# Queries of two pairs in one run, one E buffer of two tiles: a lambda convolution on Trainium2

## The reference

```python
softmax_keys = jax.nn.softmax(keys, axis=1)
values = _bn(xf @ Wv.T, gamma_v, beta_v, axes=(0, 2), ch_shape=(1, -1, 1))
queries = _bn(queries, gamma_q, beta_q, axes=(0, 2, 3), ch_shape=(1, -1, 1, 1))
content_lambda = jnp.einsum('bmk,bmv->bkv', softmax_keys, values)
position_lambdas = jnp.einsum('nmk,bmv->bnkv', E, values)
content_output = jnp.einsum('bknh,bkv->bhvn', queries, content_lambda)
position_output = jnp.einsum('bknh,bnkv->bhvn', queries, position_lambdas)
return (content_output + position_output).reshape(b, d, n1, n2)   # added to x
```

## Time and profile before

| | us |
|---|---|
| median of 3 runs | 1447.19 (1446.07 to 1447.33) |
| the profiled execution | 1447.59 |
| its span, first to last instruction | 1445.6 |
| TensorE busy | 1430.4 (99%) |
| VectorE busy | 852.0 (59%) |
| ScalarE busy | 757.0 (52%) |
| GpSimd busy | 424.6 (29%) |
| mean DMA rate | 93 GB/s |

### The profile page before, as it was taken

How to read it: one execution, slowest core, us unless ns; L and a number is a source line. 1 busy time by engine, 2 the same in 40 slices (tenths; PEclk the granted TensorE clock), 3 DMA queues, 4 the chain that set the end, 5 groups by cost and what they waited for, 6 DMA issues and landing times.

```text
span 1445.6 us, 36192 instructions
## 1 busy us (share of the span) xinstructions
PE 1430.4 (99%) x14608; PEld 1191.8 (82%) x14608; DVE 852.0 (59%) x1226; ACT 757.0 (52%) x1109; POOL 424.6 (29%) x366
## 2 busy tenths in 40 slices
PE   8999999999999999999999999999999999999998
PEld 7997888888888888888888888888888888888886
DVE  7989565555555555555555555555555555555553
ACT  6775555555455555554555455544555455545552
POOL 6683233223322332133212331233223322332130
PEclk9999999999999999999999999999999999999999
DMA  8845322434152422434152333424252333425221
GB/s 308 289 156 93 84 66 66 87 94 94 40 120 65 110 63 75 93 93 89 44 123 65 95 65 87 94 75 85 65 123 65 72 80 94 94 53 107 65 58 30
DMA packets 342684, 134.68 MB, mean 93 GB/s; under 512 B 206864, under 2 KB 338048, under 8 KB 342144
## 3 DMA queue, kind: packets, MB, share of 16 engines
q1 hardware_dynamic: 342656, 134.31, 38.6%
HBM read 109.12 MB, written 25.17 MB: 93 GB/s over the span
## 4 chain that ended last, share of the span: by engine, by line
PE 97%; DVE 1%; DMA 0%; issue 0%; ACT 0%; SPq 0%; POOL 0%; POOLq 0%; DVEq 0%
PE ps_a L1224 81%; PE ps_b L1241 5%; PE ps_a L1208 4%; PE ps_b L1104 3%; PE ps_a L1094 1%; PE ps_b L1163 1%; DMA x_main<-in_x 0%; DVE bn L719 0%; DVE q_stats L744 0%; DVE v_stats L738 0%; DVE key_diag L782 0%; POOL v_rstd L459 0%; PE ps_b L1179 0%; DVE top_level L774 0%; DVE top_level L773 0%
## 5 line engine op out<-in xcount | busy, mean ns | idle before, releaser
L1224 PE MATMUL ps_a<-v_hi,e_hi 128*128 128x512 f32 x1708 | 670.8, 393 | 0.0
L1224 PE MATMUL ps_a<-v_hi,e_lo 128*128 128x512 f32 x1708 | 664.7, 389 | 0.0
L657 ACT ACTIVATE q_diag<-q_blk,q_shift_n,q_scale_n 128x256 f32<-128x256 f32 x512 | 411.2, 868 | 42.9 <-PE ps_b L1241 42.9
L575 ACT ACTIVATE e_hi<-e_nat 128x512 fp32r<-128x512 f32 x305 | 192.8, 633 | 442.2 <-PE ps_a L1224 435.6
L1224 PE MATMUL ps_a<-b_lo,e_hi 128*128 128x512 f32 x976 | 379.6, 389 | 0.0
L1224 PEld LDWEIGHTS ps_a<-v_hi,e_hi 128*128 128x128 f32 x1708 | 320.5, 188 | 67.3
L1224 PEld LDWEIGHTS ps_a<-v_hi,e_lo 128*128 128x128 f32 x1708 | 320.7, 188 | 64.7
L486 POOL TENSOR_TENSOR e_nat<-e_nat,s_buf 128x512 f32<-128x512 f32 x61 | 79.7, 1306 | 920.2 <-DVE e_lo L749 920.2
L854 DVE TENSOR_TENSOR pos<-ps_a,content 128x512 f32<-128x512 f32 x183 | 126.6, 692 | 296.0 <-PE ps_a L1224 296.0
L749 DVE TENSOR_TENSOR e_lo<-e_nat,e_hi 128x512 fp32r<-128x512 f32 x305 | 290.7, 954 | 1.7 <-ACT e_hi L575 1.4
L1224 PE MATMUL ps_a<-t_lo,e_hi 128*128 128x512 f32 x732 | 285.4, 390 | 0.0
(11 more groups left out here) (133 smaller groups left out, 890.3 us busy)
## 6 DMA issues: line engine op xcount, KB each, us to landing
e_nat<-in_L_conv_E SPq DMA_DIRECT2D x128, 512.0 KB, 4.8
res<-in_x SPq DMA_DIRECT2D x64, 256.0 KB, 5.9
out_dram<-res SPq DMA_DIRECT2D x60, 256.0 KB, 4.7
x_main<-in_x SPq DMA_DIRECT2D x24, 512.0 KB, 6.0
q_dram<-q_nat SPq DMA_DIRECT2D x4, 2048.0 KB, 7.6
q_blk<-q_dram SPq DMA_DIRECT2D x32, 256.0 KB, 2.9
x_more<-in_x SPq DMA_DIRECT2D x8, 512.0 KB, 8.6
out_dram<-res SPq DMA_DIRECT2D x4, 192.0 KB, 3.7
```

Of the source, the lines that this page charges most:

```text
L575: nc.scalar.activation(e_hi[:, i], e_source(i, slot), ACT.Copy).then_inc(e_hi_ready, 1)
L657: ins = nc.scalar.activation(to[:, n], of, ACT.Identity, bias=q_shift_n[:, n:n + 1], scale=q_scale_n[:, n:n + 1])
L1224: ins = nc.tensor.matmul(BANK_OF[i], e[:, i, j].rearrange("p n k -> p (n k)"), v[:, j], start=(STARTS[i] and j == 0 and n == 0), stop=(STO ...
```

## The change

It runs the queries of pairs 2g and 2g+1 as one stretch of 128 matmuls (256 records), behind product 0 of pair 2g+2 (`query_group`), for g = 1 to 30. Queries 0, 1, 62 and the halves of 63 stay apart. For this `q_diag` and `pos` are held for two pairs, the sums are added with one instruction (`add_group`, from both banks of ps_b), and `res` is held for two groups of two pairs. To make room, `e_nat` shrinks from two slots to one: tile 1 of the next pair is loaded after split 5, tile 0 after split 6 (`next_e`), each with its own semaphore.

In odd pairs, where no query stands behind product 0, product 0 goes to bank_d and product 1 starts bank_a anew; VectorE adds product 0 into `head` and also, with content, into the two places of `pos` in which it is needed (two more additions). VectorE's and ScalarE's orders in a pair are changed: additions out of PSUM come ahead of splits, and a part of `norm_queries` ahead of each split. TensorE's loop now has two pairs in its body.

```diff
-        e_nat = sb("e_nat", [P, 2, 2 * TN, J * KD])
+        e_nat = sb("e_nat", [P, 2 * TN, J * KD])
-        res = sb("res", [P, G * NH, 2 * BN])
-        q_diag = sb("q_diag", [P, 2, B * NH * TN])
+        res = sb("res", [P, G * NH, 2, GN])
+        q_diag = sb("q_diag", [P, 2, 2, B * NH * TN])
-        pos = sb("pos", [P, 2, BV])
+        pos = sb("pos", [P, 2, 2, BV])
...
-        BANK_OF = (bank_a, bank_a, bank_b, bank_a, bank_c, bank_a, bank_b)
-        STARTS = (True, False, True, False, True, False, False)
+        BANK_OF = ((bank_a, bank_a, bank_b, bank_a, bank_c, bank_a, bank_b),
+                   (bank_d, bank_a, bank_b, bank_a, bank_c, bank_a, bank_b))
+        STARTS = ((True, False, True, False, True, False, False), (True, True, True, False, True, False, False))
...
+            def next_e(p):
+                sp.wait_ge(e_lo_ready, p * NP + NP - 1)
+                load_e(p + 1, 1)
+                sp.wait_ge(e_lo_ready, p * NP + NP)
+                load_e(p + 1, 0)
...
+            def even_loads(p, grp, half):
+                next_e(p)
+                sp.wait_ge(res_added, p)
+                store_res(grp - 1, 1 - half)
+
+            def odd_loads(p, grp, half, queries=True):
+                next_e(p)
+                sp.wait_ge(res_stored, grp * (16 * A))
+                load_res(grp + 1, 1 - half)
+                if queries:
                     sp.wait_ge(q_diag_ready, p + 1)
-                    load_q(blk * 2 + i // 2 + 2, i // 2)
+                    load_q(grp + 2, half)
...
+            def e_sums(p, first=False):
+
+                pool.wait_ge(e_loaded[1], p * 16 + 16)
                 if not first:
                     pool.wait_ge(e_lo_ready, p * NP - NP + 3)
+                pool.tensor_tensor(s_buf[:, 0], e_block(1, 0), e_block(1, 1), ALU.add).then_inc(s_ready, 1)
                 pool.wait_ge(s_ready, p * 4 - 4 * PLAIN + 1)
+                pool.wait_ge(e_loaded[0], p * 16 + 16)
...
-                    if not (isinstance(p, int) and p == 0):
+                    if i % 2 == 0 and not (isinstance(p, int) and p == 0):
                         act.wait_ge(queried, p)
...
                     for n in range(NP - 1):
-                        split_hi(p + 1, n, (i + 1) % 2)
                         norm_queries(p, i, PARTS[n])
+                        split_hi(p + 1, n)
...
-                nc.vector.tensor_tensor(head[:], bank_a, content[:, 0:BC], ALU.add).then_inc(evacuated, 1)
+                ins = nc.vector.tensor_tensor(head[:], BANK_OF[odd][0], content[:, 0:BC], ALU.add)
+                if odd:
+                    for t in range(2):
+                        ins = nc.vector.tensor_tensor(pos[:, odd, t, BC:BV], bank_d, content[:, BC:BV], ALU.add)
+                ins.then_inc(evacuated, 1)
...
+            def add_group(p, half):
+
+                dve.wait_ge(res_loaded, p * (8 * A) + 16 * A)
+                dve.wait_ge(queried, p + 2)
+                r = res[:, :, half].rearrange("v f (t n) -> v f t n", t=4)
+                s = ps_b[:, 0].rearrange("v (t f n) -> v f t n", t=4, n=TN)
+                nc.vector.tensor_tensor(r, s, r, ALU.add).then_inc(res_added, 2)
...
+            def pair(p, i, last=False):
+                odd = i % 2
+                evacuate_c12(p - 1, 1 - odd)
+                split_lo(p, 6)
+                evacuate_head(p, odd)
+                if last:
+                    add_out(p - 1)
+                elif not odd:
+                    add_group(p - 2, 1 - i // 2)
+                evacuate_u2(p, odd)
                 if not last:
+                    split_lo(p + 1, 0)
+                    split_lo(p + 1, 1)
+                evacuate_u3(p, odd)
+                evacuate_c22(p, odd)
                 if not last:
+                    split_lo(p + 1, 2)
+                evacuate_c11(p, odd)
                 if not last:
+                    split_lo(p + 1, 3)
+                evacuate_c21(p, odd)
                 if not last:
+                    split_lo(p + 1, 4)
+                    split_lo(p + 1, 5)
...
-            EVACUATED_BEFORE = (-1, 1, 0, 2, -2, 3, 4)
+            EVACUATED_BEFORE = ((-1, 1, 0, 2, -2, 3, 4), (-1, -1, 0, 2, -2, 3, 4))
...
+            def query_group(p):
+
+                pe.wait_ge(evacuated, p * NP + 2 * NP)
+                pe.wait_ge(q_diag_ready, p + 2)
+                pe.wait_ge(res_added, p)
+                query_images(0, 0)
+                query_images(1, 1).then_inc(queried, 2)
...
-            pair(PLAIN, first=True)
-            with pe.Fori(PLAIN + 1, PAIRS - 1) as p:
-                pair(p)
-            product(PAIRS - 1, 0, False)
+            def pairs(p):
+                product(p, 0, 0)
+                query_group(p - 2)
                 for i in range(1, NP):
+                    product(p, 0, i)
+                for i in range(NP):
+                    product(p + 1, 1, i)
+
+            for i in range(NP):
+                product(PLAIN, 1, i, first=True)
+            with pe.Fori(2, GROUPS - 1) as grp:
+                pairs(grp * 2)
+            product(PAIRS - 2, 0, 0)
+            query_group(PAIRS - 4)
```

More of the change, by code:

```diff
@@ L1025, in _ @@
             evacuate_first(2)
[L1026 to L1038 removed]
+            split_lo(PLAIN, 3)
@@ L1213, in plain_sums, with product @@
                 return ins
-            def product(p, i, first, js=range(MJ)):
+            def product(p, odd, i, first=False, js=range(MJ)):
                 pe.wait_ge(e_lo_ready, p * NP + i + 1)
-                pe.wait_ge(evacuated, p * NP + (EVACUATED_BEFORE[i] if i or not first else 4 - NP))
+                pe.wait_ge(evacuated, p * NP + (EVACUATED_BEFORE[odd][i] if i or not first else 4 - NP))
                 if first and i in (1, 2, 3, 5):
```

309 lines of the change are left out of this document (145 added, 164 removed).

## The result

The changed kernel takes **1444.23 us** (median of 15 runs, 1441.83 to 1445.38), the kernel before 1447.14 us on the same chip (15 runs, 1445.67 to 1447.36): a ratio of 0.998 with a 95% interval of 0.9972 to 0.9987. It is faster, by 2.9 us. Forecast were 1435.8 us and a gain of 11.4; the measured time lies above the whole range. The profiled execution took 1445.38 us for a span of 1443.3; it is the slowest of the 15.

What follows compares the result with a forecast made beforehand. The prediction took TensorE, busy 99% of the 1445.6 us span, to bound the kernel. Thirty merges at 0.38 us gave 11.4 us off the median 1447.19, all other terms 0: 1435.8 us, range 1433.0 to 1439.5.

Steps and rivals of the forecast that it cites:

- Merged queries, 0.38 us each, 11.4 in all: TensorE's pair loop: 30 switches between wide and 32-column matmuls disappear; gain 11.4 us, bounds 10.2 to 12.6.
- A longer loop body: TensorE's loop body grows from 424 to 848 instructions; taken as 0, bounds 0 and 2.9 us per turn.
- rival 1: TensorE's loop: the longer body is fetched again at each turn, 84 us over 29 turns, about 1520 us; chance 0.06.
- The clock: TensorE in the longer group: a lower clock was put under rival 3; earlier light work had not lowered it.
- rival 3: Grouped queries: merging saves little, or the clock drops in the longer group; within 3 us of 1447; chance 0.05.
- Prologue: Before the loop: the later E loads of pairs 1 and 3 are covered; 0, with 1.5 us either way.
- bank_d at 0: Product 0 of odd pairs: bank_d avoids a wait of some 0.9 us per odd pair; cost on the path 0.
- E in one buffer: E loads in the loop: later loads still arrive in time, some 3.2 us of slack in odd pairs; cost 0.
- residuals and SyncE's queue at 0: Grouped residual additions on VectorE, and twice as many half-size residual transfers in SyncE's queue; each costed at 0.
- Rival 4: Odd pairs or prologue: short waits lose part of the gain, say half, giving 1441.5 us; chance 0.07.
- The range: Whole kernel: 1433.0 to 1439.5 us, from the gain's bounds, prologue, run scatter and the nearer part of rival 4.
- The sign of the forecast: Whole kernel: faster with chance 0.85, no change 0.05, slower 0.10.

Runs made afterwards that it cites:

- experiment 6: Changed kernel with product 0 of odd pairs put back in bank_a; median 1476.71 us, ratio 1.0204 to the kernel before.
- (1): Changed kernel with 16 small unused matmuls ahead of the plain sums, shifting later code by 64 instructions; 1444.26 us, ratio 0.9983 to the kernel before.
- (7): Changed kernel with the loop's first turn written out ahead of the loop, on TensorE alone; 1446.65 us, ratio 0.9992 to the kernel before.
- (3): Changed kernel with every grouped query taken apart into two single queries, all else kept; 1447.76 us, ratio 1.0009 to the kernel before.
- (8): Changed kernel with pair 3's query diagonals written first and pairs 60 and 61 queried singly; 1441.05 and 1440.01 us in two timings.
- experiment 2: Changed kernel with 33 small unused matmuls ahead of the plain sums, shifting later code by 132 instructions; 1447.24 us, ratio 1.0005 to the kernel before.

## Why the prediction was wrong

- **Merged queries, 0.38 us each, 11.4 in all**: right. 0.397 us by the turns' length, 11.9 in all. That the fixed part of a query is tied to the switch and not to its records held in every turn from the second on, and the grouped query takes 2.63 us between starts of products, as forecast.
- **"A longer loop body", taken as 0**: this is the step that failed. I asked only whether the body would be fetched again at each turn (rival 1). It isn't: between 260 and 1390 us the trace has no packet on TensorE's instruction queue,

```profile
DMA packets 403091, 94.15 MB, mean 83 GB/s; under 512 B 290449, under 2 KB 403089, under 8 KB 403089
...
q1 hardware_dynamic: 403089, 94.13, 37.7%
q14 instruction: 2, 0.02, 0.0%
```

  so that 848 instructions stay where they are, and turns 2 to 29 cost nothing. (q14 is not counted: its two packets of 8 KB are too few for a body that would be fetched again at each turn.) What I didn't ask is how fast new code comes on its first pass, when 512 instructions in a row are gone in 2.2 us. The earlier trace rows had the 18 fetches, and the earlier trace rows the speed of the records. 3.6 us of stop in the first group and 2.15 us in the last (with its small gap) are this. The argument "turns of the old body show no cost at all" was about resident code, and about queries half as long.
- **The clock**, which rival 3 brushed aside with the earlier trace rows (0.47 of 2.10 us busy at 1.00): another 2.4 us. Light work did not lower it, and neither did the group, but it fell in the stop of 3.6 us. The row was no evidence for that case, since it was shorter and not empty. Nor is a long stop always enough: in experiment 6 the clock stayed at 1.00 through 3.58 us.
- **"Prologue", 0 with 1.5 either way**: 0.88 us lost less 0.24 won, inside the bounds. The named reason (both loads covered) was incomplete: the late one was tile 0 of pair 4, and the path led through ScalarE's queue and one of VectorE's subtractions to an addition that the first group waits for. For 20 us of cover I looked at the use of the block and not at what is queued behind it.
- **bank_d at 0**: right, and its price without was 1.13 us per odd pair, 0.9 by my sum, which counted from the end of the last matmul and not from where the next could have started.
- **E in one buffer at 0** (the step that I called riskiest), **residuals and SyncE's queue at 0**: right. In an odd pair with T at 804.0 the tile issued second was taken up by GpSimd at 810.75, T+6.7 as forecast, and block 1's subtraction ended at 812.6, T+8.6 for T+9.7:

```profile
810.75 1.29 POOL L488 TENSOR_TENSOR s_buf<-s_buf,e_nat 128x512 f32<-128x512 f32 x1 [1.85 <-DMA e_nat<-in_L_conv_E]
...
811.38 1.21 DVE L761 TENSOR_TENSOR e_lo<-e_nat,e_hi 128x512 fp32r<-128x512 f32 x1 [1.01 <-ACT e_hi L587]
```

- **Rival 4** (part of the gain lost in odd pairs or in the prologue, half: 1441.5) had the right kind, and too little of it: 9.1 us of 12 were lost before the last query. Its named places were wrong for all but 0.88 us. The sign of the forecast was right.
- **The range**: its lower end doesn't follow from its terms. 12.6, 1.5 and 1.1 us under 1447.2 make 1432.0, not 1433.0. Nothing turns on it, since the measured time lies beyond the other end.

Put right, the sum is 1447.6 - 11.9 - 0.2 + 0.9 + 3.6 + 2.4 + 2.15 = 1444.5. With the 0.7 at the end it is 1445.2, for a profiled 1445.4. That it also lies close to the median, 1444.23, is chance, as the losses are those of the slowest run.

**Shown**: that the stops belong to the place of the code (1) and to its first pass (7), that each ends 1.3 to 1.5 us after a packet of code (the 19 above), that grouping causes them (3), and that without the one behind the loop and the late start the kernel reaches 1440 to 1441 us (8). **Argued, not shown**: that the fetch of a block starts when the one before is entered. It fits 127 and 255 in experiment 2, and the packets: near 138 and 146, where the block is entered at the start of the group, they begin up to 0.4 us ahead of that matmul, while the products still run; at the later borders 0.7 to 2.4 us behind it. This delay makes the stops differ (0.9 us at 143 in the profile with 2.24, none at 146 with 1.37; 1.2 at 219, 2.2 in the changed kernel), and what sets it is open. Other traffic may (DMA share 0.82 in the stop of the changed kernel); that was not tried alone. Open too is when a stop lowers the clock.

## What to carry to other kernels

Short instructions in long rows are cheap only in code that has run before. In a first pass, count how fast a block of 256 instructions is consumed: here 1.1 us of 32-column matmuls against a fetch that left 1 to 4 us of stop, once in each group of new code, and in most of the longer ones another 1.4 to 2.4 us for a lower clock. So a merge that pays 0.40 us in each turn of a loop is a loss in straight code: group inside the loop, and leave what is executed once in smaller pieces between long instructions. And when a buffer is dropped, follow the later load not to its use alone but through every queue that its consumers stand in.

## What the runs showed of the hardware

- TensorE stood still for 3.40 us within a row of matmuls that wait for nobody, while one block of 16 KB of code was fetched (213.63 to 214.68 us; TensorE went on at 216.05). The fetches are blocks of 256 instructions: adding 64 instructions moved the stop by 32 records, and borders lay 128 records apart. The Trainium skill ("Runtime: NRT & Kernel Launch", section "Instruction fetch mechanics") gives just this block, and says that the cost of crossing one is mostly hidden because instructions are dispatched more slowly than blocks come. For products this trace agrees, as no stop stands within the loop's first 168 of them (the small one of 0.3 us is behind the loop); for 32-column matmuls, two instructions in 0.0085 us, it doesn't, by up to 3.9 us a block.
- The Trainium skill's warning in the same section, of a stall at taken branches outside a window of two blocks, is not borne out for TensorE: 848 instructions, over three blocks, are looped over with no fetch in 1130 us. The room for 2048 instructions that the section gives TensorE fits.
- The granted clock went to half in or behind 12 of the 13 stops of 2.49 to 3.93 us in the table, and stayed at 1.00 at the thirteenth (3.58 us, experiment 6) and at the six of 0.96 to 2.24 us. In the changed kernel it came back 5.5 us after work resumed (216.0 to 221.5) and cost 2.4 us; behind the other stops in first turns it cost 1.4 to 1.7 us. It also differs from run to run: of the 15 runs of the changed kernel, the two with a mean clock of 1.000 took 1441.8 and 1442.9 us, the median one, at 0.997, 1444.2; but those at 0.998 took from 1442.3 to 1444.8, so that it isn't all of the scatter.
